# A two-layer mixer on one core: two big products as seven block products instead of eight in three of four batch groups, with their weights' sums and parts kept in HBM

## The reference

```python
x = x + _L0_ffn_ref(_L0_cond_ref(x, cond_128, ...), L0_ffn_weight, L0_ffn_bias, lora_A, lora_B, starts)
x = x + _L1_ffn_ref(_L1_cond_ref(x, cond_128, W0, b0, W1, b1, W2, b2, weight, bias_k), A, B, Wr)
```

## Time and profile before

| | |
|---|---|
| median of three runs | 687.66 us |
| profiled execution, its own time | 687.75 us |
| its span, first to last instruction | 686.0 us |
| PE busy | 680.1 us (99%) |
| DVE busy / ACT busy / POOL busy | 320.6 (47%) / 184.9 (27%) / 61.7 (9%) |
| DMA queues | 90.30 MB, mean 132 GB/s |
| granted TensorE clock | 0.999 |

### The profile page before, as it was taken

How to read it: one execution, slowest core, us unless ns; L and a number is a source line. 1 busy time by engine, 2 the same in 40 slices (tenths; PEclk the granted TensorE clock), 3 DMA queues, 4 the chain that set the end, 5 groups by cost and what they waited for, 6 DMA issues and landing times.

```text
span 686.0 us, 8649 instructions
## 1 busy us (share of the span) xinstructions
PE 680.1 (99%) x3341; PEld 564.7 (82%) x3341; DVE 320.6 (47%) x533; ACT 184.9 (27%) x238; POOL 61.7 (9%) x91
## 2 busy tenths in 40 slices
PE   9999999999999999999999999999999999999997
PEld 8878888888987888888898888888889788888886
DVE  2824563723543266463273327564337233647333
ACT  2612232421222132332221213332113211324211
POOL 1585000000003300000000510000000000000000
PEclk9999999999999999999999999999999999999999
DMA  8394115524471202553265130363416112035242
GB/s 296 106 369 169 61 32 170 175 93 154 155 275 63 92 32 65 165 161 129 103 241 201 65 104 2 99 204 112 162 64 253 61 61 92 31 118 194 94 153 92
DMA packets 30101, 90.30 MB, mean 132 GB/s; under 512 B 3328, under 2 KB 4224, under 8 KB 29952
## 3 DMA queue, kind: packets, MB, share of 16 engines
q1 hardware_dynamic: 24608, 78.84, 33.5%
q10 hardware_dynamic: 5472, 11.19, 5.1%
HBM read 81.08 MB, written 8.93 MB: 131 GB/s over the span
## 4 chain that ended last, share of the span: by engine, by line
PE 98%; DMA 1%; ACT 0%; DVE 0%; ACTq 0%; issue 0%; DVEq 0%
PE bank L828 26%; PE bank L830 26%; PE bank L829 26%; PE bank L857 8%; PE bank L928 4%; PE bank L908 2%; PE bank L887 1%; PE bank L889 1%; PE bank L939 1%; PE bank L938 1%; DMA toep<-taps 1%; PE bank L969 0%; PE bank L977 0%; DVE piece_lo L602 0%; ACTq L225 0%; ACT piece_hi L440 0%
## 5 line engine op out<-in xcount | busy, mean ns | idle before, releaser
L602 DVE TENSOR_TENSOR piece_lo<-raw,piece_hi 128x1024 fp32r<-128x1024 f32 x99 | 123.8, 1254 | 225.4 <-ACT piece_hi L440 225.3
L828 PE MATMUL bank<-piece_hi,u_hi 128*128 128x512 f32 x512 | 202.5, 396 | 0.1
L830 PE MATMUL bank<-piece_hi,u_lo 128*128 128x512 f32 x512 | 202.0, 395 | 0.0
L829 PE MATMUL bank<-piece_lo,u_hi 128*128 128x512 f32 x512 | 201.9, 394 | 0.0
L440 ACT ACTIVATE piece_hi<-raw 128x1024 fp32r<-128x1024 f32 x99 | 104.8, 1058 | 297.1 <-PE bank L830 290.2
L828 PEld LDWEIGHTS bank<-piece_hi,u_hi 128*128 128x128 f32 x512 | 96.5, 189 | 22.9 <-issue 0.5
L830 PEld LDWEIGHTS bank<-piece_hi,u_lo 128*128 128x128 f32 x512 | 96.4, 188 | 22.5
L829 PEld LDWEIGHTS bank<-piece_lo,u_hi 128*128 128x128 f32 x512 | 96.5, 189 | 22.3
L828 PE MATMUL bank<-v_hi,piece_hi 128*128 128x512 f32 x256 | 101.9, 398 | 0.0
L830 PE MATMUL bank<-v_hi,piece_lo 128*128 128x512 f32 x256 | 101.1, 395 | 0.0
L829 PE MATMUL bank<-v_lo,piece_hi 128*128 128x512 f32 x256 | 101.0, 394 | 0.0
(11 more groups left out here) (111 smaller groups left out, 393.2 us busy)
## 6 DMA issues: line engine op xcount, KB each, us to landing
raw<-pieces SPq DMA_DIRECT2D x99, 512.0 KB, 3.4
conv_in<-conv_x SPq DMA_DIRECT2D x16, 516.0 KB, 6.2
x<-x SPq DMA_DIRECT2D x16, 512.0 KB, 5.2
gate_x<-gates ACTq DMA_DIRECT2D x32, 256.0 KB
out<-x SPq DMA_DIRECT2D x32, 256.0 KB, 2.3
mixb_bc<-spread ACTq DMA_DIRECT2D x1, 1024.0 KB, 4.9
cond_bc<-spread ACTq DMA_DIRECT2D x1, 768.0 KB, 9.6
x<-lora_b SPq DMA_DIRECT2D x1, 512.0 KB, 12.7
```

Source lines behind the costliest of these rows:

```text
L602: dve.tensor_tensor(piece_lo[:, n % SLOTS, :], raw[:, n % SLOTS, :], piece_hi[:, n % SLOTS, :].bitcast(F32), ALU.subtract).then_inc(s_piec ...
L828: pe.matmul(to, left_hi, right_hi, start=first, stop=False)
L829: pe.matmul(to, left_hi, right_lo, start=False, stop=False)
L830: return pe.matmul(to, left_lo, right_hi, start=False, stop=last)
```

## The change

Group 0 computes as before, with pieces split on the core. It also prepares for the others. With the 1024 x 1024 weight in 2 x 2 blocks of 512 x 512, VectorE forms the four sums that the Winograd form of Strassen's product needs (`combine`, in place in `work`), four operations for each of two units per weight; they are split in parts (`combined_hi`, `combined_lo`, into `v_hi` and `v_lo`) and written to `kept` in HBM by `keep_weights`. The eight pieces of the experts' first product are written as parts by `keep_piece`.

Groups 1 to 3 take 36 steps each. A step is one piece in both parts. Steps 0 to 13 are the first layer's seven products (`winograd`, two steps each, 24 matmuls a product), 14 to 21 the eight pieces of `h`, 22 to 35 the last layer's seven products. 12 steps are loaded raw (`RAW`) and split as before; 24 are fetched from `kept` as two parts (`KEPT`, two DMAs of 512 KB). `SLOTS` is 4 for parts, `RAWS` 2 for raw pieces. The activations' blocks need four sums per layer on VectorE (`sums`), parts of them (`sums_hi`, `sum_lo`), and additions of the products to four quarters of the output, some through `partial`. The `ring` of three becomes `work`, which holds all eight. ScalarE, VectorE and SyncE have an extra copy of the program for the last group, TensorE does not. `cond_bc` and `mixb_bc` hold one group and are reloaded.

```diff
 LORA_M = LORA_LO + LORA
 KC = 8
 PIECES = 24
-SLOTS = 3
-RING = 24
+SLOTS = 4
+RAWS = 2
+ITEMS = 24
+QUARTER = TOK // 2
+STEPS = 36
+RAW = {0: 0, 1: 1, 2: 2, 3: 3, 8: 6, 9: 7, 22: 16, 23: 17, 24: 18, 25: 19, 32: 22, 33: 23}
+KEPT = {4: 0, 5: 1, 6: 4, 7: 5, 10: 2, 11: 3, 12: 6, 13: 7, **{n: n - 6 for n in range(14, 22)},
+        26: 22, 27: 23, 28: 16, 29: 17, 30: 20, 31: 21, 34: 18, 35: 19}
+RAW_AT = {n: r for r, n in enumerate([*RAW, STEPS, STEPS + 1, STEPS + 2, STEPS + 3])}
+S1, S2, S3, S4 = 0, 1, 2, 3
+CHUNKS = (4, 5, 6, 7, 0, 1, 2, 3)
 LAG = 3
 WARM_UP = 12
 GATES = 4
...
+        work = sb("work", [P, NCH, TOK])
+        partial = sb("partial", [P, 2, HALF])
...
+        def step_used(eng, g, n):
+            if n < 14:
+                eng.wait_ge(s_win, g * 42 + (3 * (n // 2) + (1, 3)[n % 2] - 42))
+            elif n < 22:
+                eng.wait_ge(s_h, g * NCH + n - 13)
+            else:
+                eng.wait_ge(s_win, g * 42 + (3 * (n // 2 - 4) + (1, 3)[n % 2] - 42))
...
+        def quarter(th, kh):
+            return work[:, 4 * kh:4 * kh + 4, th * QUARTER:(th + 1) * QUARTER]
+        def sum_part(part, i):
+            return part[:, 2 * i:2 * i + 2, :].rearrange("p a (b c) -> p (a b) c", c=QUARTER)
+        def weights(tile, i):
+            return tile[:, 2 * i:2 * i + 2, :].rearrange("p a n -> p (a n)")
...
+            def keep_piece(n):
+                sp.dma_start(kept[n, 0], piece_hi[:, n % SLOTS, :].bitcast(F32)).then_inc(s_kept[n % SLOTS], 16)
+                sp.dma_start(kept[n, 1], piece_lo[:, n % SLOTS, :].bitcast(F32)).then_inc(s_kept[n % SLOTS], 16)
+            def fetch(g, n):
+                step_used(sp, g, n - SLOTS)
+                sp.dma_start(piece_hi[:, n % SLOTS, :].bitcast(F32), kept[KEPT[n], 0]).then_inc(s_fetched[n % SLOTS], 16)
+                sp.dma_start(piece_lo[:, n % SLOTS, :].bitcast(F32), kept[KEPT[n], 1]).then_inc(s_fetched[n % SLOTS], 16)
...
+                def load_weights(base, unit, i):
+                    piece = base + (0, 4, 2, 6)[i] + unit
+                    sp.dma_start(weights(work, i), pieces[piece]).then_inc(s_comb_in[i], 16)
+                def keep_weights(base, unit, i, step):
+                    at = base + 2 * (0, 1, 3, 2)[i] + unit
+                    sp.wait_ge(s_sum_lo, step)
+                    sp.dma_start(kept[at, 0], weights(v_hi, i).bitcast(F32)).then_inc(s_comb[i], 16)
+                    sp.dma_start(kept[at, 1], weights(v_lo, i).bitcast(F32)).then_inc(s_comb[i], 16)
...
+                next_raw(21)
+                sp.wait_ge(s_lo, H0 + NCH)
+                for i in range(4):
+                    load_weights(16, 0, i)
+                next_raw(22)
+                next_raw(23)
+                for step, i in enumerate((0, 1)):
+                    keep_weights(16, 0, i, 9 + step)
+                    load_weights(16, 1, i)
+                next_raw(24)
+                for step, i in enumerate((3, 2)):
+                    keep_weights(16, 0, i, 11 + step)
+                    load_weights(16, 1, i)
+                for t in range(NT):
+                    store(0, t, 0, t + 1)
+                next_raw(25)
+                next_x(0, 0, 0)
+                next_x(0, 1, 0)
+                for step, i in enumerate((0, 1)):
+                    keep_weights(16, 1, i, 13 + step)
+                next_raw(26)
...
+                next_raw(24)
+                next_raw(25)
+                fetch(g, 26)
+                next_raw(32)
+                fetch(g, 27)
+                next_raw(33)
+                for n in range(28, 31):
+                    fetch(g, n)
+                for t in range(2):
+                    store(g, t, 0, 3 + t)
+                fetch(g, 31)
...
+            def sums_hi(g, at):
+                for i, done in ((S1, 1), (S2, 3), (S4, 4), (S3, 4)):
+                    act.wait_ge(s_sum, g * 8 + (8 + at + done))
+                    of = (quarter(1, 1), quarter(0, 0), quarter(1, 0), quarter(0, 1))[i]
+                    act.activation(sum_part(v_hi, i), of, ACT.Copy).then_inc(s_sum_hi, 1)
...
+                split_first(4)
+                mix_bias()
+                for step, i in enumerate((0, 1, 3, 2)):
+                    combined_hi(0, i, step + 1)
+                split_first(5)
+                split_first(6)
+                lora_parts(0)
...
+                def combine(unit):
+                    for i in range(4):
+                        dve.wait_ge(s_comb_in[i], 16 * (unit + 1))
+                    b11, b12, b21, b22 = (weights(work, i) for i in range(4))
+                    dve.tensor_tensor(b11, b12, b11, ALU.subtract).then_inc(s_sum, 1)
+                    dve.tensor_tensor(b12, b22, b12, ALU.subtract).then_inc(s_sum, 1)
+                    dve.wait_ge(s_sum, 4 * unit + 2)
+                    dve.tensor_tensor(b22, b22, b11, ALU.subtract).then_inc(s_sum, 1)
+                    dve.wait_ge(s_sum, 4 * unit + 3)
+                    dve.tensor_tensor(b21, b21, b22, ALU.subtract).then_inc(s_sum, 1)
+                def combined_lo(unit, step):
+                    i = (0, 1, 3, 2)[step]
+                    dve.wait_ge(s_sum_hi, 4 * unit + step + 1)
+                    if unit:
+                        dve.wait_ge(s_comb[i], 32 * unit)
+                    dve.tensor_tensor(weights(v_lo, i), weights(work, i), weights(v_hi, i).bitcast(F32),
+                                      ALU.subtract).then_inc(s_sum_lo, 1)
...
+                split_first(4)
+                combine(0)
+                combined_lo(0, 0)
+                combined_lo(0, 1)
+                split_first(5)
+                combined_lo(0, 2)
+                combined_lo(0, 3)
+                split_first(6)
+                masked(0, 4)
+                lora_rest(0)
...
+                split_first(20)
+                combine(2)
+                split_first(21)
+                for step in range(3):
+                    combined_lo(2, step)
+                split_first(22)
+                combined_lo(2, 3)
+                for t in range(NT):
+                    dve.wait_ge(s_fin, t + 1)
+                    add(banks[t][:, :], t, 0, s_o)
+                dve.wait_ge(s_o, 4)
+                dve.sem_inc(s_o, 6)
+                split_first(23)
+                combine(3)
+                combined_lo(3, 0)
+                combined_lo(3, 1)
+                split_raw(0, STEPS)
+                combined_lo(3, 2)
+                combined_lo(3, 3)
+                split_raw(0, STEPS + 1)
+                split_raw(0, STEPS + 2)
+                for t in range(NT):
+                    dve.wait_ge(s_fin, NT + t + 1)
+                    add(banks[4 + t][:, :], t, 1, s_o)
+                dve.wait_ge(s_o, 14)
+                dve.sem_inc(s_o, 8)
+                for i in range(4):
+                    dve.wait_ge(s_comb[i], 32 * 4)
...
+            def group(g, last):
+                def sums(at):
+                    step = g * 8 + (8 + at)
+                    dve.tensor_tensor(quarter(1, 1), quarter(1, 0), quarter(1, 1), ALU.add).then_inc(s_sum, 1)
+                    dve.tensor_tensor(quarter(1, 0), quarter(0, 0), quarter(1, 0), ALU.subtract).then_inc(s_sum, 1)
+                    dve.wait_ge(s_sum, step + 2)
+                    dve.tensor_tensor(quarter(0, 0), quarter(1, 1), quarter(0, 0), ALU.subtract).then_inc(s_sum, 1)
+                    dve.wait_ge(s_sum, step + 3)
+                    dve.tensor_tensor(quarter(0, 1), quarter(0, 1), quarter(0, 0), ALU.subtract).then_inc(s_sum, 1)
+                def sum_lo(at, i):
+                    done = (1, 2, 4, 3)[i]
+                    dve.wait_ge(s_sum_hi, g * 8 + (8 + at + done))
+                    of = (quarter(1, 1), quarter(0, 0), quarter(1, 0), quarter(0, 1))[i]
+                    dve.tensor_tensor(sum_part(v_lo, i), of, sum_part(v_hi, i).bitcast(F32),
+                                      ALU.subtract).then_inc(s_sum_lo, 1)
...
+                split_raw(g, 23)
+                gated(g, 7, H_BANKS[7])
+                gated_lo(g, 7)
+                split_raw(g, 24)
+                dve.wait_ge(s_lo, g * ITEMS + ITEMS)
+                sums(4)
+                split_raw(g, 25)
+                for s in range(2):
+                    first_product(1, s)
+                    add(partial[:, s, :], s, 0, s_o)
+                sum_lo(4, S1)
+                sum_lo(4, S2)
+                for s in range(2):
+                    won(dve, g, 1, 1, s)
+                    read(s_o, 1 + s)
+                    add(banks[4 + s][:, :], s, 0, s_o)
...
+                def winograd(n, to, hi, lo, rows, stop):
+                    for j in range(2):
+                        if n + j in RAW:
+                            raw_ready(n + j)
+                        else:
+                            fetched(n + j)
+                        for s in range(2):
+                            for c in range(2):
+                                k = 2 * j + c
```

(44 more changed lines are left out.)

1275 lines of the change are left out of this document (819 added, 456 removed).

## The result

| | before | after |
|---|---|---|
| median, same chip, 4 runs each | 687.44 us | 703.63 us (702.72 to 707.29) |
| profiled execution | 687.75 us | 703.15 us |
| its span | 686.0 us | 701.4 us |

The ratio is 1.0247, 95% interval 1.0201 to 1.0293. The forecast was 684.5 us, 668 to 696: wrong in sign and outside its range. One of the four runs before took 3867.35 us; the ratio is taken without it. The largest part of the difference is one wait, shown now.

The account below looks back on a forecast made before the run. The prediction took TensorE, busy 99% of the span, as the bound: matmul count times spacing, new waits added in full. -33.5 + 9.3 + 11.5 + 3 + 4.7 + 1.8 = -3.2 gave 684.5 us, range 668 to 696.

Parts of the forecast that it names:

- Removed matmuls, -33.5: Both layers of groups 1 to 3: 144 fewer matmuls at 0.2325 us each save 33.5 us.
- The LoRA, +9.3: Group 0, first layer: ten VectorE operations ahead of the LoRA mask make TensorE wait 9.3 us more.
- The other end, 12.6: High end of the LoRA term: each VectorE operation waits out a whole GpSimd operation, +12.6 us.
- The junction, +11.5: End of group 0: late additions to x stall TensorE at group 1's third convolution item, 11.5 us.
- Its high end, 16 us: Upper bound of the stall at group 0's end, for transfers at only 0.26 MB/us.
- Rate after idling, +3: After the two long TensorE waits, slower matmuls cost 1.5 us each, 3 us in all; ends 0 and 4.2.
- Step 25, +4.7: Last layer of groups 1 to 3: step 25's low part comes 1.5 to 1.6 us late each, 4.7 us.
- Fetches, 0: Groups 1 to 3: fetching kept steps costs nothing while the rate is above 0.31 MB/us.
- Tail, +1.8: After the last matmul: three additions in place of one precede the last store, 1.8 us more.
- Rival 1: The gain arrives: store chain off the path, TensorE waits only for the LoRA; 665.7 us, chance 0.20.
- Rival 2: Port lock: GpSimd blocks VectorE for whole operations, 12.6 for 9.3, and the clock costs 4.2; 689 us, chance 0.12.
- Rival 3: Slower than before: fetches bound groups 1 to 3, at steps 26 to 35; 709 us, chance 0.07.

Follow-up runs that it names:

- e8: The changed kernel without group 0's preparation for the last product; groups 1 to 3 fetch the first layer's kept pieces instead: 676.07 us, ratio 0.9828 to the kernel before.
- e2: The changed kernel with GpSimd's mixing of group 0's matrices held until the LoRA mask is done: 701.77 us, ratio 1.0199 to the kernel before.
- e3: The changed kernel with group 1's convolution input (2 MB) loaded between pieces 8 and 9 of group 0, not behind piece 12: 699.44 us, ratio 1.0184.
- e9: The changed kernel without group 0's preparation for the first layer; groups 1 to 3 fetch the last product's pieces instead: 695.77 us, ratio 1.0121.
- e5: The changed kernel with step 25's split ahead of the four sums of the last product in groups 1 to 3: 698.86 us, ratio 1.0173.
- e13: e12 with step 3's split behind the seventh convolution item and step 37's load issued beside step 36's: 679.80 us, ratio 0.9883 to the kernel before.
- e12: The changed kernel with the moves of e1, e3, e5 and e11 together, nothing left out: 687.31 us, ratio 0.9999 to the kernel before.
- e1: The changed kernel with group 0's LoRA mask and parts ahead of the first unit's low parts and pieces 5 and 6: 701.99 us, ratio 1.0214.
- e4: The changed kernel with splits of steps 36 and 37, additions and step 37 and 38 loads moved ahead at group 0's end, store wait later: 702.16 us.
- e7: The changed kernel with the last unit's four weight loads issued ahead of the 4 MB of stores of the unit before: 702.51 us, ratio 1.0223.
- e11: e7 plus step 38's load ahead of the last stores, additions ahead of the last two low parts, and a later wait for stores: 699.96 us.

## Why the prediction was wrong, step by step

**Removed matmuls, -33.5: right.** The page has 144 fewer (3341 to 3197), and from 249.70 to 261.78 us their spacing is 0.232. e8 shows that most of the time arrives. Its profiled execution is 8.3 us shorter than before's (679.40 to 687.75); the waits it has more than before (9.6 at the LoRA, 4.9, 1.5, 1.2) and the tail of 1.7 add up to 18.9, and the clock behind the LoRA wait is about 2. Together 29; where the other 4 us went is not shown.

**The LoRA, +9.3: right.** 10.5 against 1.0 before is +9.5. The mask ran at 56.00, the sum said 55.6; the operations took 1.53 to 1.76, it took 1.55. The other end, 12.6, did not come; e2 shows that GpSimd is the cause of the 1.55 (1.22 without it).

**The junction, +11.5: the step that failed.** It measured +23.6. Against the prediction's milestones, counted from the end of h (194.84, the first convolution item, less eight pieces of 5.58 and 1.7 of late pieces: 148.5 us):

| | predicted | measured |
|---|---|---|
| piece 19's low part done | +3.7 | +11.4 |
| first sums start | +12.5 | +21.3 |
| `combine(3)` starts | +41 | +53.0 |
| last split (step 38) done | +57.7 | +71.2 |
| additions done | +60.2 | +73.6 |
| TensorE wants them | +48 | +50.1 |

Of the 13.4 us at the additions 7.7 are there at the first line, so what failed first is the start of the chain. The prediction took "+3.7" from the earlier trace rows, where VectorE waited 2.03 us for TensorE at the last chunk and not for a transfer. (That row is piece 18's low part; with three slots piece 19's came at 142.27, with four it stands in that place.) It asked what the new work delays on VectorE, ScalarE and SyncE, and never what new stores in the DMA engines do to ScalarE's small transfers, `gates` and `gate_x`. Before, ScalarE's two issues and VectorE's first gated chunk:

```profile
108.23 0.53 ACTq L501 DMA_DIRECT2D gates<-gate_t  x1
...
110.54 2.56 ACTq L495 DMA_DIRECT2D gate_x<-gates  x4
```

```profile
115.28 0.69 DVE L735 TENSOR_TENSOR ring<-bank,gate_x 128x512 f32<-128x512 f32 x1 [4.11 <-DMA gate_x<-gates]
```

After:

```profile
119.71 0.54 ACTq L651 DMA_DIRECT2D gates<-small  x1
...
125.70 2.74 ACTq L656 DMA_DIRECT2D gate_x<-gates  x4
```

The `gates` store took 6.0 us until `gate_x` could be issued, where it had taken 2.3, and the first `gate_x` 9.7 (125.7 to 135.4), where it had taken 4.8 (110.5 to 115.3). The first gated chunk stood 20.2 us ahead of the end of h before and 13.1 after: 7.1 us lost, and the last chunk kept them (0.1 behind the end of h before, 7.8 after).

The convolution input, in the same engines at the same time, is a part of it: without it (e3) the two transfers took 3.3 and 7.0 us, but only 2.4 us were left of the gain at the first sums (+18.9 for +21.3), as later `gate_x` and a raw piece (1.36 us) were waited for in their turn. The first layer's stores have none that shows: in e9 the two transfers took 5.6 and 9.4 us. What is left are the 8 MB of kept pieces 8 to 15, stored just there, and the raw pieces, which have two slots in place of three. The share of 0.91 to 1.03 from 128 to 136 us speaks for the stores, but no run took them away.

Between the first line and the first sums 1.1 us more are lost, and 3 us in the chain of stores and loads (32 us from sums to sums, against 28.5). VectorE itself was idle for most of it (14.13 us in one piece).

The bound was wrong too. Its high end, 16 us, was drawn from one cause, the transfer rate, and the rate came near what was taken: 381 GB/s from 180 to 200 us and 318 at a share of 0.86 from 200 to 220, against 0.40 MB/us. What was not in the range was that the chain could start late. The sum also puts a landing at 1.9 us beside its transfer, where its own figures give 2.1 (3.4 less 1.3); that is 0.2 us each time.

**Rate after idling, +3: right in size.** The granted clock was 0.50 until about 62 and 226 us; TensorE worked for some 4 us at half rate after each stretch and lost 2 each time, 4 us. The high end (4.2) was nearer, and with it what the Trainium skill says in "TensorE: Matmul & The Clock Gate", Part 1: after idling the clock falls to 1.2 GHz. The trace agrees: 0.50 is that level (matmuls with 512 columns came 0.43 us apart from 59.24 to 61.80, 0.23 behind).

**Step 25, +4.7: 3.6**, and e5 shows that nothing is late behind it. **Fetches, 0: 1.2. Tail, +1.8: 1.7**, from the last matmul's start to the end of the span (5.6 against 3.9). **Not in the sum:** 2.8 us for the late pieces of group 0, of which the first is at 142.62, in the middle of the late `gate_x` (e3 removes both).

Measured sum: -33.5 + 9.5 + 23.6 + 2.8 + 4 + 3.6 + 1.2 + 1.7 = 12.9, against 15.4 between the two spans. 2.5 us stay open.

**The rivals.** Rival 1 (the store chain is off the path, 665.7) did not come; even e8, which has no such chain, took 676.07. Rival 2's price for the lock (12.6) did not come either, though its clock did; that VectorE and GpSimd exclude each other is not refuted (e2). Rival 3 named the right resource, DMA, and a result over 701, but the wrong place: groups 1 to 3 waited 1.2 us for fetches in all. The queue that it placed there stood in group 0.

**What stays open.** The part of the kept pieces' stores and of the raw pieces' two slots, above. Whether the order of e13 can be bettered, and how much of its 7.7 us at the junction is DMA bandwidth (from 184 to 216 us the engines are nearly full in e12 as well), was not tried.

## What to carry to other kernels

When work that only prepares later stages is put into a full schedule, follow the one queue it uses, and list everything that stands behind it there, small transfers of other engines included; a milestone read from the old trace holds only if nothing new stands ahead of it. A wait does not end by moving the operation that is named in it: here three moves alone (e1, e4, e7) each brought under 2 us, since VectorE, working in order, met the next late transfer, and a wait that is cut in parts can leave TensorE at half rate between them (e11); take out what is blocked early and needed late (step 3's split) first. Leaving a whole preparation out (e8, e9) prices it in one run, and should come before any fine experiment.

## What was not expected of the hardware

- SyncE's issue of a 512 KB transfer took 0.33 to 0.48 us where it was quickest, and 0.45 to 1.9 us from 180.86 us on, while the DMA engines' share was 0.98 to 1.02. The ten issues from 180.86 to 190.76 held SyncE for 9.9 us, and with it the next load.
- VectorE's 128 x 1024 operations with two inputs in SBUF took 1.22 us alone and 1.53 to 1.76 beside GpSimd.
- Between 184 and 200 us stores and loads mixed at 345 to 417 GB/s, not far from the loads alone in the earlier trace rows (396 and 402).
